# A gated cross-attention and expert layer on Trainium2: all four down tiles of a quad moved in front of its last two products

## The chip, the cores and the metric

The kernel runs on one core of a Trainium2 chip. The core has a matrix engine (TensorE, PE in the profile, with its weight loads as PEld), VectorE (DVE), ScalarE (ACT), GpSimd (POOL) and SyncE (SP), which issues most of the DMA. Each engine works through its own list of instructions in order and waits on semaphores where it needs another's result. The metric is the device time of one execution in microseconds; lower is better.

## The reference

What is computed, cut to what matters here (8 sequences of 256 tokens, width 512; 8 expert groups with 352 inner features each):

```python
x = x + tanh(g_xattn[0]) * xattn(layernorm(x), ctx, ctx, wq, wk, wv, wo)      # keys: 256 context + 256 own tokens
x = x + tanh(g_ffn[0]) * ffn(layernorm(x), ...)

def ffn(x):                                     # x: 2048 tokens x 512
    scores = softmax(x @ gate_w.T)              # 64 experts
    topk_w, topk_idx = top_k(scores, 8)
    w_e = zeros.at[rows, topk_idx].add(topk_w)
    flat = w_e[:, inv_map]                      # 8 groups of 8
    scalar = flat.sum(-1)
    soft = softmax(where(flat == 0, -1e9, flat), axis=-1)
    xg = x[:, None, :] + einsum('ngi,ghi->ngh', soft, mask_up_w)
    g = einsum('ngh,gih->ngi', xg, gate_proj_w)
    u = einsum('ngh,gih->ngi', xg, up_proj_w)
    d = einsum('ngi,ghi->ngh', silu(g) * u, down_proj_w)
    return einsum('ng,ngh->nh', scalar, d)
```

All matrix products are made from operands split into a high and a low part, three matmuls (low by high, high by low, high by high) per block of 128.

## The kernel before

The attention part and the router run first, one sequence at a time, up to about 340 us. Then comes the expert part, in which the change lies. It has two passes over 1024 tokens each. A pass has eleven units, a unit is two quads, so there are 44 quads (0 to 43; 0 to 21 are the first pass, 22 to 43 the second). One quad takes 128 inner features of the gate and of the up projection for two chunks of 512 tokens. The four half-size block products of either are made with seven products in place of eight, by sums and differences of weights and tokens. Each of the seven is six matmuls of 128x128 by 128x512 (line 1605).

**A quad on TensorE.** Products 1 and 6, in the first pass eight small matmuls for the masked stack (line 1619), products 2, 5 and 7, two small-stack matmuls (line 1611, "soft"), product 4 with a soft matmul, product 3 with a soft matmul. Beside them each quad carries four of the eight down tiles of the unit before it (line 76, six matmuls each): an even quad tiles 0 to 3, an odd one tiles 4 to 7. `early_tiles` says how many of these four stand behind the soft pair, in front of product 4; the rest stand behind product 3. Before the change that is two and two. Quads 0, 1, 2 and 43 have none early.

**What the other engines do with it.** There are two sets of buffers and PSUM banks, for even and odd quads.
- ScalarE copies product 1 out of PSUM (`first_sum`, line 921; product 2 waits for it), makes the two silus (lines 977 and 997), and rounds weights (line 796) and activations (`act_high`, line 889) to their high halves. At an even quad it also rounds the down weights (line 904).
- VectorE adds the products (lines 1316, 1348, 1355, 1398, 1404), multiplies (1401, 1413) and scales (line 1297), adds each down tile to the residual (`add_down`, line 1304), and in the first pass masks the small stack (lines 1277 to 1288) and does the router's steps for the last sequences. `add_down` of a tile stands where the tile does: early ones in front of the wait for product 4, of the late ones the third tile's behind line 1404 and the fourth's behind the last scaling.
- GpSimd makes weight sums (lines 640 to 645), the low halves of the weights (649), of the down weights (694) and of the activations (`act_low`, line 699), and in quads 11, 13, 15 and 17 sums of a piece of the tokens (lines 658 to 667).
- SyncE loads the weights of quad q + 2 once the last low half of quad q is made, and stores the router's scalars (line 429) in quads 2, 9 and 14, in one queue with the loads.

**What waits for what around the change.** The last group of a quad's weights is rounded on ScalarE only when the previous quad's product 3 is done, and in the first pass the small matmuls wait for its low half. Product 5 waits for line 1277, the soft pair for line 1288. The first down tile of an even quad waits for the low halves of the down weights and of an activation block (`act_low` of the quad before), and each down tile waits for the residual add two tiles before it, as there are two PSUM banks for them.

Of the kernel before, what the change touches and what calls it, by code (L numbers as in the profile page):

```python
# [28 lines left out]
QUADS = 2 * UNITS  # L29
# [31 lines left out]

def early_tiles(q):

    return 0 if q <= 2 or q == QUADS - 1 else 2


def split_products(hi_l, lo_l, hi_r, lo_r, tiles):
# [52 lines left out]
def layer_program(nc, x, ctx_nat, ctx_t, w_qkvo, w_gate_up, w_down, mask_up, gate_t, inv_map, gains, out):  # L120
    with ExitStack() as stack:
# [119 lines left out]
        early = Zone(a.at)  # L241
# [157 lines left out]
        def _(sp):  # L399
# [56 lines left out]
            def store_piece(i):  # L456
                _, _, at = piece_tokens(i)
                sp.wait_ge(s_piece_lo, i + 1)
                for dram, part in ((th_dram, sums_hi), (tl_dram, sums_lo)):
                    sp.dma_start(dram[:, :, :, at:at + PIECE].rearrange("p t k n -> p (t k) n"),  # L460
                                 f32(part[piece_home(i)][:]).rearrange("p c k n -> p (c k) n")).then_inc(s_piece_out, 16)
# [542 lines left out]
        def _(dve):  # L1004
# [286 lines left out]
            def scaled(quad, c, part):  # L1291

                q = quad.q
                dve.wait_ge(s_prod, 2 * q + c + 1)
                if quad.p == 0:
                    dve.wait_ge(s_scal_in[quad.j], 16 * HALF_G * (quad.s + 1))
                nc.vector.tensor_tensor(part, part, scalars[:, quad.j, c], ALU.mult).then_inc(s_act, 1)  # L1297

            def add_down(n):

                u, t = divmod(n, UNIT_TILES)
                row = xres[:, u // PAIRS * UNIT_TILES + t, :]
                dve.wait_ge(s_down, n + 1)
                nc.vector.tensor_tensor(row, row, bank[6 + t % 2][:], ALU.add).then_inc(s_res, 1)  # L1304
# [14 lines left out]
            for quad in quads:  # L1319
                q = quad.q  # L1320
                sums = tmp[quad.set]
                psum_b, psum_c = bank[BANKS[quad.set][1]], bank[BANKS[quad.set][2]]
                below = 4 * (q - 2)
                early = early_tiles(q)

                if q != 1:
# [85 lines left out]
                dve.wait_ge(s_c22, q + 1)  # L1412
                nc.vector.tensor_tensor(sums[:, SUM_3], sums[:, SUM_3], sums[:, SUM_2], ALU.mult).then_inc(s_prod, 1)  # L1413
                scaled(quad, 1, sums[:, SUM_3])
                if q >= 2:
                    add_down(below + 3)
            for n in range(UNIT_TILES * (UNITS - 1), UNIT_TILES * UNITS):
                add_down(n)
# [2 lines left out]
        def _(pe):  # L1421
# [266 lines left out]
            def soft_products(quad):  # L1688
                q, s, j = quad.q, quad.s, quad.j
                psum_a, _, psum_c = banks_of(quad)  # L1690
                if s == 0:
                    pe.wait_ge(s_a_st, q + 1)
                else:
                    pe.wait_ge(s_a_in[j], 16 * (quad.p + 1))
                if quad.p == 0:
                    pe.wait_ge(s_soft_in[j], 16 * (s + 1))
                soft_product(psum_c, quad, UP, 1).then_inc(s_m5, 1)
                soft_product(psum_a, quad, GATE, 0).then_inc(s_c11, 1)
# [50 lines left out]
            for quad in quads[2:]:  # L1749
                q = quad.q  # L1750
                below = 4 * (q - 2)
                early = early_tiles(q)
                product_1(quad)
                product_6(quad)
# [100 lines left out]
```

## Time and profile before

| | |
|---|---|
| median of 3 runs | 1096.89 us (1096.8 to 1097.58) |
| the profiled execution's own time | 1099.27 us |
| its span, first to last instruction | 1097.5 us |
| TensorE busy | 1056.5 us, 96% |
| VectorE / ScalarE / GpSimd busy | 746.9 / 379.8 / 634.1 us |
| mean granted TensorE clock | 0.989 of full speed |
| HBM read and written | 79 MB and 32 MB |

The span is about 1.8 us shorter than that execution's time, and the execution is 2.4 us longer than the median of the runs. A busy share says how much an engine works, not whether its results come in time: in an ordered queue one late result stops all behind it.

### The profile page before, as it was taken

What the parts mean: (1) busy time and instruction counts of PE and PEld (TensorE: products, weight loads), DVE (VectorE), ACT (ScalarE), POOL (GpSimd) and SP (SyncE); (2) the same over time, 40 slices, a digit from 0 to 9 for tenths busy, and PEclk for the clock granted to TensorE, in tenths of its full rate; (3) what the DMA queues carried; (4) which work ended last, traced back from release to release, by engine and by line L of the source; (5) the groups of instructions that cost most, each with busy time, mean ns of one, the idle gap of its engine ahead of it and who ended that gap; (6) DMA issues with size and microseconds to landing.
All of it is one profiled execution on the core that took longest, in us unless ns stands there. A gap on an engine that the chain in (4) does not pass through costs nothing.

```text
span 1097.5 us, 14456 instructions
## 1 busy us (share of the span) xinstructions
PE 1056.5 (96%) x5388; PEld 895.8 (82%) x5388; DVE 746.9 (68%) x1320; ACT 379.8 (35%) x635; POOL 634.1 (58%) x511
## 2 busy tenths in 40 slices
PE   7999999999999869999999999999999999999998
PEld 7889988988887657888877788878888888888886
DVE  7775665766667845878788988746656655665665
ACT  4333323433323333334244333323233333323331
POOL 0212203533515826866888888756777776677761
PEclk8999999999999998999999999999999999999999
DMA  9112225356685252023332633294322112212202
GB/s 333 61 40 96 60 47 145 65 157 164 176 249 176 77 54 73 28 81 46 92 104 60 125 110 121 80 324 137 105 73 72 43 57 73 72 47 71 72 27 77
DMA packets 114134, 111.64 MB, mean 102 GB/s; under 512 B 20881, under 2 KB 96401, under 8 KB 114065
## 3 DMA queue, kind: packets, MB, share of 16 engines
q1 hardware_dynamic: 113696, 110.58, 35.2%
q8 instruction: 43, 0.70, 0.3%
q14 instruction: 27, 0.21, 0.1%
q10 hardware_dynamic: 368, 0.15, 0.1%
HBM read 79.05 MB, written 31.65 MB: 101 GB/s over the span
## 4 chain that ended last, share of the span: by engine, by line
PE 76%; DVE 12%; DMA 3%; issue 3%; SPq 2%; ACT 2%; POOL 1%; DVEq 0%; ACTq 0%
PE bank L76 40%; PE bank L1605 29%; PE bank L1611 3%; PE bank L1438 1%; DVE a_stack L1288 1%; DVE tmp L1297 1%; DMA wgu_raw<-in_w_gate_up 1%; PE bank L1619 1%; SPq L460 1%; DVE tmp L1413 1%; DVE xres L1304 1%; DMA x2t<-token_sums_l 1%; DVE tmp L1401 1%; DVE a_stack L1286 1%; DVE soft L1137 1%
## 5 line engine op out<-in xcount | busy, mean ns | idle before, releaser
L1605 PE MATMUL bank<-x2t,wgu_hi 128*128 128x512 f32 x1144 | 354.2, 391 | 0.0
L649 POOL TENSOR_TENSOR wgu_lo<-wgu_raw,wgu_hi 128x512 fp32r<-128x512 f32 (+1 forms) x129 | 210.4, 1637 | 97.5 <-ACT wgu_hi L796 95.8
L1605 PEld LDWEIGHTS bank<-x2t,wgu_hi 128*128 128x128 f32 x1144 | 215.7, 189 | 44.4
L1605 PE MATMUL bank<-x2t,wgu_lo 128*128 128x512 f32 x572 | 225.6, 394 | 5.6 <-DMA x2t<-token_sums_l 2.7
L796 ACT CAST wgu_hi<-wgu_raw 128x512 fp32r<-128x512 f32 (+1 forms) x129 | 93.7, 727 | 231.4 <-PE bank L1611 188.9
L1304 DVE TENSOR_TENSOR xres<-xres,bank 128x512 f32<-128x512 f32 x176 | 120.0, 682 | 54.6 <-PE bank L76 54.5
L1605 PEld LDWEIGHTS bank<-x2t,wgu_lo 128*128 128x128 f32 x572 | 107.9, 189 | 30.6 <-issue 4.9
L76 PE MATMUL bank<-wd_hi,at_second 128*128 128x512 f32 x336 | 130.8, 389 | 0.0
L76 PE MATMUL bank<-wd_hi,at_first 128*128 128x512 f32 x256 | 99.9, 390 | 2.4 <-issue 2.4
L1297 DVE TENSOR_TENSOR tmp<-tmp,scalars 128x512 f32<-128x512 f32 x88 | 99.1, 1127 | 3.0
L1348 DVE TENSOR_TENSOR tmp<-tmp,bank 128x512 f32<-128x512 f32 x44 | 30.2, 686 | 94.8 <-PE bank L1605 94.2
L694 POOL TENSOR_TENSOR wd_lo<-wd_raw,wd_hi 128x512 fp32r<-128x512 f32 x42 | 54.2, 1312 | 54.2 <-ACT wd_hi L904 54.2
L76 PE MATMUL bank<-xnt_hi,w_lo_qkv 128*128 128x256 f32 x256 | 75.0, 293 | 2.6 <-DVE xnt_lo L1049 2.6
L76 PEld LDWEIGHTS bank<-wd_hi,at_second 128*128 128x128 f32 x336 | 63.1, 188 | 13.3
L76 PE MATMUL bank<-xnt_hi,w_hi_qkv 128*128 128x256 f32 x256 | 73.6, 288 | 0.0
L76 PE MATMUL bank<-xnt_lo,w_hi_qkv 128*128 128x256 f32 x256 | 73.6, 287 | 0.0
L1611 PE MATMUL bank<-soft_t,a_stack 128*128 128x512 f32 x176 | 62.9, 398 | 3.5 <-DVE a_stack L1288 3.4
L977 ACT ACTIVATE tmp<-bank 128x512 f32<-128x512 f32 x44 | 26.3, 599 | 114.2 <-PE bank L1611 114.2
L76 PE MATMUL bank<-wd_lo,at_second 128*128 128x512 f32 x168 | 65.4, 389 | 0.0
L699 POOL TENSOR_TENSOR at_second<-tmp,at_second 128x512 fp32r<-128x512 f32 x44 | 59.9, 1380 | 5.7 <-ACT at_second L889 5.7
L699 POOL TENSOR_TENSOR at_first<-tmp,at_first 128x512 fp32r<-128x512 f32 x33 | 45.3, 1374 | 29.1 <-ACT at_first L889 29.1
L76 PEld LDWEIGHTS bank<-wd_hi,at_first 128*128 128x128 f32 x256 | 48.2, 188 | 13.7 <-issue 2.8
(213 smaller groups left out, 2253.5 us busy)
## 6 DMA issues: line engine op xcount, KB each, us to landing
wgu_raw<-in_w_gate_up SPq DMA_DIRECT2D x43, 512.0 KB, 4.2
wd_raw<-in_w_down SPq DMA_DIRECT2D x22, 512.0 KB, 4.9
a_stacks<-a_stack SPq DMA_DIRECT2D x22, 192.0 KB, 1.9
a_stack<-a_stacks SPq DMA_DIRECT2D x22, 192.0 KB, 4.0
ctxt_raw<-in_ctx_t SPq DMA_DIRECT2D x8, 512.0 KB, 11.7
ctx_raw<-in_ctx SPq DMA_DIRECT2D x8, 512.0 KB, 9.4
x<-x_raw SPq DMA_DIRECT2D x8, 512.0 KB, 4.0
sums_raw<-x SPq DMA_DIRECT2D x16, 256.0 KB, 3.9
```

What stands on the lines that cost most here:

```text
L76: last = nc.tensor.matmul(out, stationary, moving, start=n == 0, stop=n == len(pairs) - 1)
L460: sp.dma_start(dram[:, :, :, at:at + PIECE].rearrange("p t k n -> p (t k) n"), f32(part[piece_home(i)][:]).rearrange("p c k n -> p (c k) n ...
L649: nc.gpsimd.tensor_tensor(wgu_lo[:, group], raw_of(quad)[:, group], f32(wgu_hi[:, group]), ALU.subtract).then_inc(s_fw_lo, 1)
L694: nc.gpsimd.tensor_tensor(lo[:, j], wd_raw[:, j], f32(hi[:, j]), ALU.subtract).then_inc(s_wd_lo, 1)
L699: nc.gpsimd.tensor_tensor(lo, tmp[quad.set][:, SUM_3 if c else ACTED], f32(hi), ALU.subtract).then_inc(s_at_lo, 1)
L796: nc.scalar.copy(wgu_hi[:, group], raw_of(quad)[:, group]).then_inc(s_fw_hi, 1)
L977: nc.scalar.activation(sums[:, ACTED], psum_a[:], ACT.Silu).then_inc(s_silu_0, 1)
L1297: nc.vector.tensor_tensor(part, part, scalars[:, quad.j, c], ALU.mult).then_inc(s_act, 1)
L1304: nc.vector.tensor_tensor(row, row, bank[6 + t % 2][:], ALU.add).then_inc(s_res, 1)
L1348: nc.vector.tensor_tensor(sums[:, SUM_3], sums[:, SUM_1], psum_b[:], ALU.add).then_inc(s_s3, 1)
L1605: last = nc.tensor.matmul(out_bank[:], stationary, moving, start=begins and n == 0, stop=n == len(pairs) - 1, skip_group_check=True)
L1611: return nc.tensor.matmul(out_bank[:], a_stack[:, quad.j, m, :], soft_t[:, quad.j, c, :], start=False, stop=True, skip_group_check=True)
```

## The change

`early_tiles` returns 4 instead of 2 for the quads 3 to 42. On TensorE tiles 3 and 4 of the quad go in front of products 4 and 3; on VectorE their residual adds go in front of the wait for product 4, and the add that stood behind the last scaling is made only where the quad has no four early tiles. ScalarE's, GpSimd's and SyncE's lists are the same as before.

```diff
 def early_tiles(q):
-    return 0 if q <= 2 or q == QUADS - 1 else 2
+    return 0 if q <= 2 or q == QUADS - 1 else 4
@@ VectorE, behind the last scaling of a quad
-                if q >= 2:
+                if q >= 2 and early < 4:
                     add_down(below + 3)
```

TensorE before, in the second pass, from the soft matmul of product 4 in an even quad on: product 3 (line 1605), its soft matmul, then the third down tile (line 76; at_first and at_second are the two activation blocks, wd_hi and wd_lo the down weights).

```order
L1611 MATMUL bank<-soft_t,a_stack 128x512
L1605 MATMUL bank<-x2t,wgu_lo 128x512 [waits c22_done]
L1605 MATMUL bank<-x2t,wgu_hi 128x512 x2
L1605 MATMUL bank<-x2t,wgu_lo 128x512
L1605 MATMUL bank<-x2t,wgu_hi 128x512 x2
L1611 MATMUL bank<-soft_t,a_stack 128x512
L76 MATMUL bank<-wd_hi,at_first_154 128x512 [waits residual_done]
L76 MATMUL bank<-wd_lo,at_first_154 128x512
```

The same place now; x2t_spare is the token block of the next quad's product 1.

```order
L1611 MATMUL bank<-soft_t,a_stack 128x512
L1605 MATMUL bank<-x2t,wgu_lo 128x512 [waits c22_done]
L1605 MATMUL bank<-x2t,wgu_hi 128x512 x2
L1605 MATMUL bank<-x2t,wgu_lo 128x512
L1605 MATMUL bank<-x2t,wgu_hi 128x512 x2
L1611 MATMUL bank<-soft_t,a_stack 128x512
L1605 MATMUL bank<-x2t_spare,wgu_lo 128x512 [waits wgu_lo_done,silu0_done]
L1605 MATMUL bank<-x2t_spare,wgu_hi 128x512 x2
```

Behind the last matmul of product 3 the next quad's product 1 follows at once; the twelve matmuls of two down tiles that stood between them are gone from here.

VectorE before, in quad 42 of the second pass and the sum that follows it:

```order
L1355 TENSOR_TENSOR tmp_140<-tmp_140,bank 128x512 [waits m5_ready,sum3_done]
L1304 TENSOR_TENSOR xres<-xres,bank 128x512 [waits down_ready] x2
L1398 TENSOR_TENSOR tmp_140<-tmp_140,bank 128x512 [waits m4_ready]
L1401 TENSOR_TENSOR tmp_140<-tmp_140 128x512 [waits silu0_done,c21_done]
L1297 TENSOR_TENSOR tmp_140<-tmp_140,scalars 128x512 [waits prod_done]
L1404 TENSOR_TENSOR tmp_140<-tmp_140,bank 128x512 [waits m3_ready]
L1304 TENSOR_TENSOR xres<-xres,bank 128x512 [waits down_ready]
L1413 TENSOR_TENSOR tmp_140<-tmp_140 128x512 [waits c22_done,silu1_done]
L1297 TENSOR_TENSOR tmp_140<-tmp_140,scalars 128x512 [waits prod_done]
L1304 TENSOR_TENSOR xres<-xres,bank 128x512 [waits down_ready]
L1316 TENSOR_TENSOR tmp_141<-tmp_141,bank 128x512 [waits m6_ready,sum1_done]
```

and now:

```order
L1355 TENSOR_TENSOR tmp_140<-tmp_140,bank 128x512 [waits m5_ready,sum3_done]
L1304 TENSOR_TENSOR xres<-xres,bank 128x512 [waits down_ready] x4
L1398 TENSOR_TENSOR tmp_140<-tmp_140,bank 128x512 [waits m4_ready]
L1401 TENSOR_TENSOR tmp_140<-tmp_140 128x512 [waits silu0_done,c21_done]
L1297 TENSOR_TENSOR tmp_140<-tmp_140,scalars 128x512 [waits prod_done]
L1404 TENSOR_TENSOR tmp_140<-tmp_140,bank 128x512 [waits m3_ready]
L1413 TENSOR_TENSOR tmp_140<-tmp_140 128x512 [waits c22_done,silu1_done]
L1297 TENSOR_TENSOR tmp_140<-tmp_140,scalars 128x512 [waits prod_done]
L1316 TENSOR_TENSOR tmp_141<-tmp_141,bank 128x512 [waits m6_ready,sum1_done]
```

The residual adds stand in a row of four in front of the wait for product 4, and none is left between the wait for product 3 and the next quad's first sum.

## Rows read from the trace of the kernel before

**Rows 1.** One stretch, the second pass: busy time of each engine, clock, DMA.
```profile
732.00:1080.00 348.00, 344.88 (x1507) 283.36 (x1506) 211.69 (x280) 116.91 (x192) 247.99 (x211) 1.00 0.23 77
```

**Rows 2.** Chain that ended last, in quad 27: start, length, what.
```profile
824.29 2.72 PE bank L76 x12
```

**Rows 3.** Timeline (start, length, engine, line), quad 27's last matmul to quad 28's first tile.
```profile
823.90 0.39 PE L1611 MATMUL bank<-soft_t,a_stack 128*128 128x512 f32 x1
...
825.39 0.68 DVE L1404 TENSOR_TENSOR tmp<-tmp,bank 128x512 f32<-128x512 f32 x1
...
827.49 0.69 DVE L1297 TENSOR_TENSOR tmp<-tmp,scalars 128x512 f32<-128x512 f32 x1
...
828.44 0.59 ACT L921 COPY tmp<-bank 128x512 f32<-128x512 f32 x1 [1.71 <-PE bank L1605]
828.93 0.62 ACT L889 CAST at_second<-tmp 128x512 fp32r<-128x512 f32 x1
...
830.15 2.54 POOL L694 TENSOR_TENSOR wd_lo<-wd_raw,wd_hi 128x512 fp32r<-128x512 f32 x2 [3.52 <-ACT wd_hi L904]
832.65 2.54 POOL L699 TENSOR_TENSOR at_second<-tmp,at_second 128x512 fp32r<-128x512 f32 x2
...
834.17 0.40 PE L76 MATMUL bank<-wd_hi,at_first 128*128 128x512 f32 x1
```

**Rows 4.** Timeline, behind the last matmul of quad 26.
```profile
807.96 0.39 PE L1611 MATMUL bank<-soft_t,a_stack 128*128 128x512 f32 x1
...
810.08 0.63 ACT L997 ACTIVATE tmp<-tmp 128x512 f32<-128x512 f32 x1 [1.06 <-DVE tmp L1404]
...
811.16 0.62 ACT L889 CAST at_first<-tmp 128x512 fp32r<-128x512 f32 x1 [0.46 <-PE bank L76]
...
811.86 1.29 POOL L699 TENSOR_TENSOR at_first<-tmp,at_first 128x512 fp32r<-128x512 f32 x1 [0.57 <-ACT at_first L889]
811.87 1.83 DVE L1297 TENSOR_TENSOR tmp<-tmp,scalars 128x512 f32<-128x512 f32 x1
```

**Rows 5.** Timeline, small matmuls and VectorE's mask in quad 21.
```profile
712.50 0.28 PE L1619 MATMUL bank<-wgu_hi,mu 128*128 128x256 f32 x1
...
713.09 0.67 DVE L1316 TENSOR_TENSOR tmp<-tmp,bank 128x512 f32<-128x512 f32 x1
...
713.45 0.40 PE L1605 MATMUL bank<-x2t,wgu_lo 128*128 128x512 f32 x1
...
713.69 0.41 DVE L1277 TENSOR_TENSOR a_tmp<-bank,group_mask 128x256 f32<-128x256 f32 x1
```

**Rows 6.** Timeline, last matmul of quad 7 and VectorE's add of it.
```profile
478.85 0.39 PE L1611 MATMUL bank<-soft_t,a_stack 128*128 128x512 f32 x1
...
481.90 0.68 DVE L1404 TENSOR_TENSOR tmp<-tmp,bank 128x512 f32<-128x512 f32 x1
```

**Rows 7.** Timeline of GpSimd, first and last operation of a token piece.
```profile
586.43 1.19 POOL L658 TENSOR_TENSOR sums_raw<-sums_raw 128x256 f32<-128x256 f32 x1
...
589.68 1.07 POOL L667 TENSOR_TENSOR sums_raw<-sums_raw 128x256 f32<-128x256 f32 x1
```

**Rows 8.** Timeline, the load for quad 5 and quad 4's wait.
```profile
396.49 0.60 SPq L438 DMA_DIRECT2D wgu_raw<-in_w_gate_up  x1
...
409.57 0.72 POOL L640 TENSOR_TENSOR wgu_raw<-wgu_raw 128x256 f32<-128x256 f32 x1 [15.05 <-DMA wgu_raw<-in_w_gate_up]
...
413.83 0.55 PE L1619 MATMUL bank<-wgu_hi,mu 128*128 128x256 f32 x1 [11.26 <-POOL wgu_lo L649]
```

**Rows 9.** Waits of TensorE over the span: us in total, times, longest.
```profile
PE bank L1611 <- DVE a_stack L1288: 3.4, 7, 1.3
```

**Rows 10.** Timeline of TensorE behind two waits.
```profile
377.32 0.47 PE L76 MATMUL bank<-wd_hi,at_first 128*128 128x512 f32 x1 [2.39 <-issue]
...
734.99 0.68 PE L1605 MATMUL bank<-x2t,wgu_lo 128*128 128x512 f32 x1 [2.70 <-DMA x2t<-token_sums_l]
...
738.46 0.41 PE L76 MATMUL bank<-wd_hi,at_first 128*128 128x512 f32 x1
```

## The prediction

> **What bounds the kernel now.** I read the stretches first, then the critical chain of one quad, then the timeline of all engines around the end of a quad's last product. In the stretch of the second pass TensorE is busy 344.9 of 348 us at the full clock while the Vector, Scalar and GpSimd engines are busy 212, 117 and 248 us [rows 1]. So matmul issue bounds this stage: the twelve matmuls of two down tiles take 2.72 us, or 0.227 us each [rows 2]. No other engine is short of time in sum; whether one of them is late at some point of a quad is a question of slack, and that is where the change acts. The number of matmuls stays the same, so TensorE can win nothing but waits that exist now, and it has few.
>
> **What is moved.** For quads 3 to 42 the third and fourth down tile leave the place behind product 3 and go in front of product 4. The last product of a quad then ends directly where the next quad begins: two down tiles, 2.72 us, of cover behind product 3 are gone. Call t0 the start of the last matmul of a quad's product 3. Everything that hangs on that product (ScalarE's second silu, the last product and scaling on VectorE, the split of the activation, and what stands behind these in the queues) had 2.72 us more before the next quad's waits than it will have. VectorE also loses two residual adds behind product 3 and gets them in front of the wait for product 4, where it was idle.
>
> **Even quads, second pass.** The first down tile of an even quad waits for the low half of the down weights and of one activation block. Behind t0 = 823.90, VectorE adds product 3 at 825.39, then silu, product and scaling; the scaling ends at 828.18, 4.28 behind t0 [rows 3]. In this trace ScalarE takes that only after the copy of the next quad's first product at 828.44, so the activation split starts at 828.93, 5.03 behind t0. From there the work is a chain: split, copies of the down weights behind it in ScalarE's queue, two subtractions on GpSimd from 830.15, the subtraction of the activation from 832.65 (half of 2.54, to 833.92), and the tile at 834.17: 5.24 us from the split's start to the tile. The tile is at t0 + 10.27 with nothing waiting. After the change it could start at t0 + 10.27 - 2.72 = 7.55. The copy on ScalarE comes 2.72 earlier too and ends at t0 + 2.4 by its own row, but the scaling does not come earlier: it hangs on product 3, and the adds that leave VectorE's queue stood in its wait for silu. So the split starts at t0 + 4.33, and the tile at 4.33 + 5.24 = 9.57. TensorE waits 2.0 us. This holds for each of ten even quads (24 to 42): 20.2 us. Below, 1.5 if the weight copies overlap better than in the row; above, 2.6 if the two subtractions meet VectorE.
>
> **Odd quads, second pass.** Here ScalarE's order behind product 3 is silu, split, copy of the next quad's first product, and product 2 waits for that copy. Behind t0 = 807.96 silu starts at 810.08, t0 + 2.12, when VectorE has added product 3. The split now waits for the fourth down tile [rows 4]; that wait goes away, but the split itself stays in the queue. Starting 0.5 us apart as ScalarE's operations do when none waits (copy and split of rows 3, 828.44 and 828.93), the split starts at 2.62 and the copy at 3.12, which ends 0.59 later at 3.71. Product 2 would start thirteen matmuls behind t0, at 2.95, and starts some 0.15 behind the copy (an estimate; rows 3 show 0.25 from 833.92 to 834.17), at 3.86: 0.91 us, eleven quads (23 to 43), 10.0 us. Below 0.4, above 1.2.
>
> **First pass.** Eight small matmuls more stand in front of product 2 (0.95 us from 712.50 to 713.45) [rows 5], so product 2 would start at 3.9 and its wait is gone, but product 5 waits for VectorE's mask of that small result. Quad by quad:
> - Odd quads: scaling, the next quad's sum and the mask follow each other on VectorE. Where GpSimd subtracts the activation at the same time, the scaling takes 1.83 instead of 0.69 us [rows 4]. It would be over at t0 + 5.3, the sum (0.67) at 5.9, the mask (0.41) at 6.25, and product 5 starts at 6.4 instead of 5.3. That is 1.1 for four quads (5, 7, 11, 21). In the other five (9, 13, 15, 17, 19) routing work or a piece of the token sums delays VectorE by 0.9 to 1.6 us, of which the small stack tile's present waits already pay a part: 1.7 each. Sum 12.9. Below 0.15 a quad, if VectorE gets its operand before GpSimd; above 2.4.
> - Even quads: as in the second pass, less the 0.95 of the small matmuls, less what transposes and present waits stand there: 0.6, 0.5 and 1.2 in quads 6, 10 and 20. In front of quad 8, VectorE's add starts 3.05 us behind t0 (478.85 to 481.90) and not 1.5 [rows 6], which leaves 1.9. In front of quads 12, 14, 16 and 18 GpSimd first makes the sums of a token piece, four operations from 586.43 to 590.75 [rows 7], and only then turns to the down weights; with these the first tile is ready at about t0 + 11.1 where it is wanted at about 8.9: 2.2 each, 8.7. Sum 12.9. Below 0.4 a quad, above 2.4.
> - Quad 4: TensorE waits 11.26 us now, until the low half of the weights is there. That chain runs back to a load which GpSimd has at 409.57. SyncE issued it at 396.49 [rows 8], behind the store of the routing scalars in its queue, and VectorE makes these scalars after its early adds. Two more adds stand in front of them, each behind its down tile: the store and the load go 2.72 us later, and the wait grows by 2.7. In quads 9 and 14 the same store moves; no product waits for the loads behind it now, and I take nothing for them (at most 2.7 each).
> - Quad 22: it waits 2.70 us for token blocks [rows 10]. The loads are bound by the queue and start behind the small stack tile of quad 21, which comes about 2 us later against TensorE: 2.0.
>
> The Trainium skill (SBUF — State Buffer, section "SBUF: two separate sides") says that VectorE and GpSimd share one port pair as an exclusive lock: whichever starts first keeps it for the whole instruction. By that rule the odd quads of the first pass keep their 1.1 us; if there were no such lock they would wait 0.15, and the sum would be 8.6 us smaller. The scaling of 1.83 us beside GpSimd's 1.29 agrees with the lock.
>
> **The sum.** 2.7 + 12.9 + 12.9 + 2.0 + 20.2 + 10.0 = 60.7 us. On the profiled execution's 1099.3 us that is 1160.0; the median of the runs lies 2.4 lower, at 1096.9, so I predict 1158. Nothing is to be set against it: TensorE's waits for the small stack tile are 3.4 us in the whole kernel [rows 9], and those hang on the same late VectorE.
>
> **Rivals.**
> - Faster. The two adds that leave VectorE's queue behind product 3 (0.68 each) shorten its chain by 1.36, the small stack tile comes earlier and its waits (3.4 us) go: 1096.9 - 3.4 = 1093.5. It decides if the scaling comes out so early that product 3 to first tile takes under 7.55 us. Against it: the chain of rows 3 adds up to 9.57, and in even quads the first of the two adds ran while silu was awaited. 3%.
> - Only the late scalars. The queues have slack that the rows hide, quads lose nothing, and the store costs 2.7: 1099.6. 6%.
> - Odd quads don't wait: ScalarE's copy gets through and VectorE wins against GpSimd. 60.7 - 10.0 - 12.9 = 37.8: 1134.7. For it: the spacing of 0.5 and the order of two operations that start within 0.02 us are all that these terms have. 15%.
> - The clock falls as well. Behind the wait of 2.70 us eight matmuls take from 734.99 to 738.46, 0.434 each and not 0.227, half the clock, so this wait costs 1.66 us on top. Behind the one of 2.39 us the clock did not fall [rows 10]. If waits of 2 us do it too, ten to twenty even quads cost 16.6 to 33.2 us more: 1174 to 1191. 12%.
>
> **How the numbers follow.** My forecast gets 64%, with a range of its own from 1143 to 1172 (the low ends of half the terms, the high ends of half). The range for 8 in 10 leaves out the two small rivals and the upper part of the clock's, and takes in the odd quads' rival: 1134 to 1176. A difference of 0.2%, 2.2 us, is about what can be told from no change. Slower by more than that: forecast, odd quads, clock and most of the late scalars, 94%. Faster 3%, within 3%.
>
> **What would show it.** Right: in each even quad of the second pass the first down tile's matmul is released by GpSimd's subtraction after some 2 us of idle time, and ScalarE's split waits for VectorE's scaling; in odd ones product 2 is released by ScalarE's copy. In the first pass product 5 waits for the mask in odd quads. The load for quad 5 is issued at about 399, and quad 4's wait is near 14. VectorE's adds stand in fours with no wait of TensorE between tiles. Wrong: TensorE gapless in the second pass, or half clock there, or waits at the down tiles for the residual adds.

## The result, and the profile after

The changed kernel takes 1142.01 us (median of 4 runs, 1141.01 to 1143.18), the kernel before 1096.85 beside it: 1.0415 times as long, 95% interval 1.0397 to 1.0433, or 45 us more. The profiled execution took 1141.01 us, its span is 1139.2 us. Of the four runs of the kernel with both orders, below, one fell in the chip's slow state (1504.12 us at a mean clock of 0.653 of full speed) and is left out there.

Page of the changed kernel, busy times; then one stretch of its second pass, with the columns of rows 1:

```profile
PE 1068.8 (94%) x5388; PEld 892.4 (78%) x5388; DVE 733.9 (64%) x1320; ACT 371.8 (33%) x635; POOL 604.5 (53%) x511
```
```profile
780.00:1110.00 330.00, 317.35 (x1372) 255.58 (x1370) 180.90 (x256) 102.24 (x176) 212.57 (x194) 1.00 0.19 63
```

TensorE stands still 12.7 of 330 us here, where it stood still 3.1 of 348 [rows 1], at the full clock. Over the span VectorE and GpSimd are busy less than before, and TensorE's busy time is 12.3 us longer for the same number of matmuls: no engine got more work, and most of what was added is waiting. TensorE's waits over the span (us in total, times, longest):

```profile
PE bank L76 <- issue: 18.2, 17, 2.4
PE bank L1619 <- POOL wgu_lo L649: 13.9, 1, 13.9
PE bank L1611 <- DVE a_stack L1288: 7.3, 11, 1.3
PE bank L1605 <- DVE a_tmp L1277: 6.6, 13, 0.9
PE bank L1605 <- ACT tmp L921: 3.8, 13, 1.1
PE bank L1605 <- DMA x2t<-token_sums_l: 3.6, 1, 3.6
```

The first row is the first down tile (one such wait of 2.4 us before, now 17 waits), the fourth is product 5 behind the mask (1.7 us before), the fifth product 2 behind ScalarE's copy (none before), the third the small stack tile [rows 9].

**Second pass, even quad.** Timeline behind the last matmul of quad 27's product 3, the place of rows 3:

```profile
853.70 0.39 PE L1611 MATMUL bank<-soft_t,a_stack 128*128 128x512 f32 x1
...
854.59 0.68 DVE L1404 TENSOR_TENSOR tmp<-tmp,bank 128x512 f32<-128x512 f32 x1
...
856.70 0.69 DVE L1297 TENSOR_TENSOR tmp<-tmp,scalars 128x512 f32<-128x512 f32 x1
...
857.43 0.63 ACT L889 CAST at_second<-tmp 128x512 fp32r<-128x512 f32 x1 [1.01 <-DVE tmp L1297]
857.96 1.13 ACT L904 CAST wd_hi<-wd_raw 128x512 fp32r<-128x512 f32 x2
...
858.65 2.53 POOL L694 TENSOR_TENSOR wd_lo<-wd_raw,wd_hi 128x512 fp32r<-128x512 f32 x2 [2.53 <-ACT wd_hi L904]
...
861.13 2.52 POOL L699 TENSOR_TENSOR at_second<-tmp,at_second 128x512 fp32r<-128x512 f32 x2
...
862.51 0.47 PE L76 MATMUL bank<-wd_hi,at_first 128*128 128x512 f32 x1 [1.08 <-issue]
862.82 0.40 PE L76 MATMUL bank<-wd_lo,at_first 128*128 128x512 f32 x1
```

The chain is the forecast one: scaling, split, weights behind it, GpSimd, tile. The tile starts at t0 + 8.81, where 7.55 was wanted: 1.26 us late, and the matmul behind it follows 0.31 us later, not 0.227. Together 1.34 us; by the length of the quad it is 1.36.

**Second pass, odd quad,** behind quad 26's product 3, the place of rows 4:

```profile
837.29 0.39 PE L1611 MATMUL bank<-soft_t,a_stack 128*128 128x512 f32 x1
...
838.91 0.64 ACT L997 ACTIVATE tmp<-tmp 128x512 f32<-128x512 f32 x1 [0.56 <-DVE tmp L1404]
...
839.45 0.60 ACT L889 CAST at_first<-tmp 128x512 fp32r<-128x512 f32 x1
...
839.95 0.57 ACT L921 COPY tmp<-bank 128x512 f32<-128x512 f32 x1
840.13 1.28 POOL L699 TENSOR_TENSOR at_first<-tmp,at_first 128x512 fp32r<-128x512 f32 x1 [0.42 <-ACT at_first L889]
840.30 1.65 DVE L1297 TENSOR_TENSOR tmp<-tmp,scalars 128x512 f32<-128x512 f32 x1
...
840.67 0.47 PE L1605 MATMUL bank<-x2t,wgu_lo 128*128 128x512 f32 x1 [0.20 <-ACT tmp L921]
```

Product 2 waits for the copy (line 921), which stands behind the split (line 889); it starts at t0 + 3.38, where 2.95 was wanted.

**First pass,** quad 21 (the place of rows 5) and quad 4 (the place of rows 8):

```profile
732.11 1.67 DVE L1297 TENSOR_TENSOR tmp<-tmp,scalars 128x512 f32<-128x512 f32 x1
...
734.30 0.41 DVE L1277 TENSOR_TENSOR a_tmp<-bank,group_mask 128x256 f32<-128x256 f32 x1
...
734.76 0.50 PE L1605 MATMUL bank<-x2t,wgu_lo 128*128 128x512 f32 x1 [0.21 <-DVE a_tmp L1277]
```
```profile
394.71 0.23 DVE L1148 TENSOR_SCALAR scal_out<-scal,gain 128x16 f32<-128x16 f32 x1
...
396.29 0.60 SPq L438 DMA_DIRECT2D wgu_raw<-in_w_gate_up  x1
...
413.57 0.55 PE L1619 MATMUL bank<-wgu_hi,mu 128*128 128x256 f32 x1 [13.93 <-POOL wgu_lo L649]
```

The load for quad 5 is issued at 396.29; that profile was 2.9 us ahead of before's at the end of quad 2, so on before's time this is 399.2. Quad 4 waits 13.93 us, not 11.26.

**The whole by quads.** A quad's length is taken from the last matmul of one product 3 to that of the next. Sums of the differences against before: quad 4 +2.9; even quads 6 to 20 +9.5; odd quads 5 to 21 +11.1; quad 22 +2.4; even quads 24 to 42 +13.6 (each 1.33 to 1.39); odd quads 23 to 43 +5.2 (0.45 to 0.49 each). That is all of the 44.7 us between the ends of quads 2 and 43; 2.7 us more in quad 3 and 2.7 less in quad 43 are the two tiles themselves, which change sides of the mark.

### The profile page after: what moved, and what is told of

Same layout as the page of the kernel before. It is cut to its first block, busy times and chain, and to the rows that moved or that the text cites. A ratio compares the mean times of both kernels' runs of the same rounds, so it can differ in the third digit from the quotient of the medians.

```text
span 1139.2 us, 14456 instructions
## 1 busy us (share of the span) xinstructions
PE 1068.8 (94%) x5388; PEld 892.4 (78%) x5388; DVE 733.9 (64%) x1320; ACT 371.8 (33%) x635; POOL 604.5 (53%) x511
## 4 chain that ended last, share of the span: by engine, by line
PE 71%; DVE 15%; issue 6%; ACT 3%; DMA 3%; POOL 2%; SPq 1%; DVEq 0%; ACTq 0%
PE bank L76 44%; PE bank L1605 21%; PE bank L1611 3%; DVE a_stack L1286 2%; PE bank L1438 2%; DVE tmp L1401 1%; DVE tmp L1398 1%; DVE tmp L1404 1%; DMA wgu_raw<-in_w_gate_up 1%; DVE a_stack L1288 1%; DVE a_tmp L1280 1%; DVE tmp L1413 1%; DMA x2t<-token_sums_l 1%; DVE tmp L1316 1%; DVE tmp L1297 1%
## 5 line engine op out<-in xcount | busy, mean ns | idle before, releaser
L649 POOL TENSOR_TENSOR wgu_lo<-wgu_raw,wgu_hi 128x512 fp32r<-128x512 f32 (+1 forms) x129 | 204.0, 1588 | 177.5 <-ACT wgu_hi L796 177.5
L1605 PE MATMUL bank<-x2t,wgu_lo 128*128 128x512 f32 x572 | 228.2, 399 | 15.1 <-DVE a_tmp L1277 6.6
L1297 DVE TENSOR_TENSOR tmp<-tmp,scalars 128x512 f32<-128x512 f32 x88 | 87.2, 991 | 3.0
L76 PEld LDWEIGHTS bank<-wd_hi,at_second 128*128 128x128 f32 x336 | 63.4, 189 | 13.5
L699 POOL TENSOR_TENSOR at_first<-tmp,at_first 128x512 fp32r<-128x512 f32 x33 | 42.5, 1289 | 29.1 <-ACT at_first L889 29.1
## 6 DMA issues: line engine op xcount, KB each, us to landing
ctxt_raw<-in_ctx_t SPq DMA_DIRECT2D x8, 512.0 KB, 11.5
```

Of the source, the lines that this page charges most:

```text
L76: last = nc.tensor.matmul(out, stationary, moving, start=n == 0, stop=n == len(pairs) - 1)
L649: nc.gpsimd.tensor_tensor(wgu_lo[:, group], raw_of(quad)[:, group], f32(wgu_hi[:, group]), ALU.subtract).then_inc(s_fw_lo, 1)
L699: nc.gpsimd.tensor_tensor(lo, tmp[quad.set][:, SUM_3 if c else ACTED], f32(hi), ALU.subtract).then_inc(s_at_lo, 1)
L1605: last = nc.tensor.matmul(out_bank[:], stationary, moving, start=begins and n == 0, stop=n == len(pairs) - 1, skip_group_check=True)
```

## The experiments

Ratios are against the kernel before, run on the same chip in turn. Its median was 1100.05 us beside the first four experiments and 1095.99 or 1096.90 beside the others, so where two experiments are compared by their times the quads' lengths in the traces are the surer measure. "q" is a quad.

### The second pass alone

```diff
-    return 0 if q <= 2 or q == QUADS - 1 else 4
+    return 0 if q <= 2 or q == QUADS - 1 else 2 if q < QUADS // 2 else 4
```

> Four early tiles in quads 22 to 42 only; quads 3 to 21 as before the change. My account by quads (measured between the ends of product 3): ten even quads of the second pass lost 1.36 us each, eleven odd ones 0.48, the rest 25.9 us lies in quads 4 to 22. Then this kernel is 18.8 us slower than before: 1115.7. Rival, that the loss of a quad is carried on from the first pass (late transfers, clock): under 8 us, below 1105.

Measured: 1118.47 us beside 1100.05, ratio 1.0173 (1.0153 to 1.0193), 19 us. Even quads 1.36 each, odd 0.48, the first pass as before. Quad 22 is 2.7 longer by the two tiles' own move and nothing else. The two passes are separate costs: these 19 us and the 25.9 of quads 4 to 22 in the changed kernel add up to the whole.

### Three tiles early

```diff
-    return 0 if q <= 2 or q == QUADS - 1 else 4
+    return 0 if q <= 2 or q == QUADS - 1 else 3
```

> Three tiles early, one late. With one tile (1.36 us) of cover behind product 3 the first tile of an even quad is wanted at t0 + 8.91 and was ready at 8.81 in the changed kernel. If the adding of product 3 stays at t0 + 0.9 as there, nothing is lost in the second pass, quad 4 loses 1.4, quads with token pieces about 0.5 each: about 1101. If it goes back to t0 + 1.49 as before the change, ten even quads lose 0.5 more: 1106. Rival, that the loss is in proportion to the tiles moved: half of 45, 1119.

Measured: 1115.11 us, ratio 1.0146 (1.0129 to 1.0163), 16 us. In the second pass as expected: 0.04 us an even quad, nothing in odd ones. The rest was a miss, as some 1101 us were expected: quads 3 and 4 lose 3.4 beside the tile's own move, not 1.4, and quads 5 to 21 of the first pass 11.0 us, the largest of them 3.6 in quad 9. There the fourth tile's add, which stays behind the last scaling, holds up a transpose of the router, and 3.4 us at half the clock follow:

```profile
506.62 1.64 DVE L1297 TENSOR_TENSOR tmp<-tmp,scalars 128x512 f32<-128x512 f32 x1
508.19 0.68 DVE L1304 TENSOR_TENSOR xres<-xres,bank 128x512 f32<-128x512 f32 x1
...
508.92 0.64 PE L1503 MATMUL bank<-ident,rest 128*64 128x128 f32 x2 [2.05 <-DVE xres L1304]
```

The cost is not proportional to the tiles moved: it starts where the cover behind product 3 falls below the chain, at another place in each pass.

### ScalarE: weights ahead of the split

The changed kernel, with the down weights rounded ahead of the activation split in even quads.

```diff
-                if q >= 1:
-                    act_high(quads[q - 1], 1)
                 if quad.j == 0 and u >= 2:
                     down_weights(u - 1)
+                if q >= 1:
+                    act_high(quads[q - 1], 1)
```

> Changed kernel, but ScalarE rounds the down weights in front of the split of the last activation block, so the GpSimd chain to the first down tile no longer hangs on VectorE's scaling. My theory: the copies start at t0 + 2.7 and not 4.3, the tile is ready at about 7.3 where it is wanted at 7.5, the even quads of the second pass win 1.36 each and plain ones of the first pass some 0.5: about 1142 - 15 = 1127. Quads 12, 14, 16, 18 stay, as GpSimd's token pieces end later. Rival, that the tile waits for the residual adds or PSUM banks: no change, 1142.

Measured: 1125.56 us, ratio 1.0231 (1.0216 to 1.0247). By the ratios 20 us of the 46 are gone, by the quads of the two traces 16.3 of 44.7, of which 13.8 lie in the even quads of the second pass; 15 were expected. Quad 28 of that kernel; its t0 is 849.34:

```profile
851.96 1.14 ACT L904 CAST wd_hi<-wd_raw 128x512 fp32r<-128x512 f32 x2
...
852.66 2.78 POOL L694 TENSOR_TENSOR wd_lo<-wd_raw,wd_hi 128x512 fp32r<-128x512 f32 x2 [0.90 <-ACT wd_hi L904]
853.08 0.62 ACT L889 CAST at_second<-tmp 128x512 fp32r<-128x512 f32 x1
...
855.39 2.54 POOL L699 TENSOR_TENSOR at_second<-tmp,at_second 128x512 fp32r<-128x512 f32 x2
...
856.89 0.39 PE L76 MATMUL bank<-wd_hi,at_first 128*128 128x512 f32 x1
```

GpSimd no longer idles behind the split, and the tile starts at t0 + 7.55 with no wait. All ten even quads lost their 1.36, odd ones kept 0.5. The even quads' wait was the order of ScalarE's queue, and of GpSimd's behind it, not work.

### ScalarE: the copy ahead of the split

The changed kernel, with `first_sum` of odd quads from 5 on ahead of `act_high`.

```diff
+                if after and q >= 4 and quad.j == 0:
+                    first_sum(after)
                 if quad.j == 0:
                     act_high(quad, 0)
```

> Changed kernel, but in front of odd quads (5 to 43) ScalarE copies the next product 1 ahead of the activation split. My theory: product 2 no longer waits (11 x 0.48 = 5.3), and GpSimd's subtraction starts 0.5 later, behind the start of VectorE's scaling, which then takes 0.7 and not 1.7, so product 5 in the first pass starts up to 0.9 earlier in nine quads (4 to 8 us): 1129 to 1133. Rival, that product 7's wait for the sum takes the place of product 2's: 1140 to 1142.

Measured: 1129.55 us, ratio 1.0275 (1.0249 to 1.0301), 15 us gone by the ratios. Odd quads of the second pass: 0.00 over before, each. Odd quads of the first pass fell from 11.1 to 2.8: with the copy first GpSimd's subtraction starts later, VectorE's scaling gets there ahead of it and ends at t0 + 3.70, not 4.66. That is 13.5 us by the quads. The profiled execution, the slowest of the four (1134.12 us), shows only 7.1 in all: its quads 12 and 16 are 1.6 and 2.2 longer than in the changed kernel, each with 3.4 us at half the clock, and quad 3 is 3.3 longer. So the rival "odd quads don't wait" was a matter of an order of two instructions, 0.5 us apart.

### Both orders

The changed kernel with both edits. Their diffs are those above.

> The changed kernel with both queue orders of the two earlier runs: ScalarE rounds the down weights ahead of the activation split in even quads, and in odd quads from 5 on copies product 1 ahead of the split. Theory: the two take away different waits, so they add up. The changed kernel stood at 1.0415 of before; the weights' order gave back 0.018, the copy's order 0.014; together about 1.009 to 1.010, some 10 us over before, of which quad 4 2.9, quad 22 2 and the rest in the first pass; second pass: even quads 0.0, odd quads 0.0 us over before. Rival (the two share a wait, so only the larger counts in a unit): 1.018 to 1.023, with 0.5 us or more left in odd quads of the second pass.

Measured: 1109.74 us (three runs), ratio 1.0119 (1.0101 to 1.0137), 13 us over before. The two add up but for 0.003, which is within the intervals; quad 12 fell to half the clock here (3.5 us over before, 1.9 in the changed kernel), which is 0.0015. One stretch of its second pass, and then VectorE and GpSimd behind quad 26's last product 3 (t0 = 822.49):

```profile
760.00:1085.00 325.00, 325.00 (x1429) 267.07 (x1427) 178.05 (x265) 109.17 (x184) 225.96 (x199) 1.00 0.20 68
```
```profile
825.50 0.69 DVE L1299 TENSOR_TENSOR tmp<-tmp,scalars 128x512 f32<-128x512 f32 x1
825.81 1.53 POOL L699 TENSOR_TENSOR at_first<-tmp,at_first 128x512 fp32r<-128x512 f32 x1 [0.89 <-ACT at_first L889]
```

TensorE has no gap left there, and of VectorE and GpSimd it is now the latter, second to start, that takes longer (1.53 us, and 1.28 in the changed kernel). What remains is the first pass (10.9 us), quad 4 (2.5) and quad 22 (2.3).

### VectorE's contention: the sums later

The kernel before, with one edit on GpSimd.

```diff
-                    if 3 <= q < QUADS - 2:
-                        weight_sums(quads[q + 2])
                     weight_low(after, 2, GROUP_C)
-                    if q < 3:
+                    if q < QUADS - 2:
                         weight_sums(quads[q + 2])
```

> The kernel before (two down tiles early), with one edit: GpSimd makes the weight sums for quad q+2 behind the low half of the last weight group and not in front of it, so that they no longer run beside VectorE's product and scaling ahead of its add of product 3. Theory (why the forecast was too long): that add stood at t0+1.49 only because two VectorE instructions in front of it ran longer beside GpSimd (0.86 and 1.12 us against 0.69). Without the sums beside them the add starts at t0+0.90, where product 3 is ready, and the scaling in even quads of the second pass ends 0.6 us earlier. The time of the whole stays within 0.3% of before in the second pass, since two tiles of cover hide it; what GpSimd makes later there may cost in the first pass. Rival (the add's time is set by product 3 or by the semaphore): the add stays at t0+1.4 to 1.5.

Measured: one run, 1105.56 us, so no interval. The second pass is within 0.02 us a quad of before. At the end of quad 27 (t0 = 830.23) the product and the scaling ahead of the add take 0.69 us each, and the add starts 0.89 behind t0; behind every product 3 from quad 23 to quad 41 it is 0.90 or within 0.01 of it:

```profile
829.79 0.69 DVE L1399 TENSOR_TENSOR tmp<-tmp 128x512 f32<-128x512 f32 x1
830.51 0.69 DVE L1295 TENSOR_TENSOR tmp<-tmp,scalars 128x512 f32<-128x512 f32 x1
831.12 0.68 DVE L1402 TENSOR_TENSOR tmp<-tmp,bank 128x512 f32<-128x512 f32 x1
```

That settles why the add was late in the trace of before. The expected gain of 0.6 us at the scaling was a miss: GpSimd's sums now stand beside the product and scaling behind the add (1.28 and 1.12 us there in place of 0.69), and the scaling ends at t0 + 4.2 to 4.8. The loss lies in the first pass's even quads (11.7 us, most of it in quads 12 to 18, where GpSimd now comes late to the down weights); quad 4 gives 3.6 back.

### Quad 4: the scalars between the adds

The changed kernel; in quad 3 VectorE makes the routing scalars between the second and the third add.

```diff
                 for n in range(early):
+                    if q == 3 and n == 2:
+                        route_scalars(B - 3)
                     add_down(below + n)
```

> The changed kernel with one edit on VectorE: in quad 3 the routing scalars of a sequence are made between the second and the third residual add, not behind all four. Theory: quad 4 waits 2.7 us longer than before only because the third and fourth add stand in front of these scalars, each behind its down tile, and the store and the load of quad 5's weights follow them in SyncE's queue. So quad 3 to quad 4 loses the 2.9 us again (with the clock up to 4 us), all other quads stay as in the changed kernel within 0.1 us: 1138 to 1139 us beside 1142. Rival (the load is late because TensorE releases the weight buffer later): quad 4 stays 2.9 us over before.

Measured: one run, 1135.99 us. Quad 4 goes from +2.9 to -0.4 us, its wait from 13.9 to 11.0. The other quads stay as they were, but for quad 16 (+1.6, a stretch at half the clock) and quad 22 (1.0 less). The predicted reason holds, shown by that one trace; 2.2 us of the total are this run's quicker early stage.

### Quad 4: the store behind the loads

The kernel before, with SyncE's store one quad later, behind the loads.

```diff
                 if q == 2:
                     store_x2(B - 1, x2r_hi, x2r_lo)
+                if q == 3:
                     store_scalars(B - 3)
```

> The kernel before (two down tiles early), with one edit: SyncE's store of a sequence's routing scalars is issued one quad later, behind the weight loads and not in front of them. Theory: quad 4's wait of 11.26 us is there because the loads of its weights stand behind the store in SyncE's queue, and the store waits for VectorE's scalars. With the store behind them the load that was issued at 396.49 comes several us earlier; quad 4's wait falls below 1 us, and the half clock behind it (10.2 us at half speed, about 5 us of cost) goes too: 11 to 15 us faster, ratio 0.986 to 0.990. Rival (the load is late for another reason, the buffer's release or GpSimd's own queue): the wait stays over 8 us, ratio 0.997 to 1.0. Second rival: the wait moves to quad 5 or 6, where the store now stands in front of another load: ratio 0.99 to 0.995 with a new wait there.

Measured: 1084.35 us beside 1095.99, ratio 0.9888 (0.9873 to 0.9904), 12 us faster than before. The load of quad 5's weights, issued at 396.49 before [rows 8], and GpSimd's first sum of them:

```profile
377.08 0.59 SPq L438 DMA_DIRECT2D wgu_raw<-in_w_gate_up  x1
...
394.27 0.73 POOL L641 TENSOR_TENSOR wgu_raw<-wgu_raw 128x256 f32<-128x256 f32 x1
```

The wait of 11.26 us is gone, quad 4 is 12.2 us shorter, and no quad behind it got longer. Quad 3 is 3.4 us longer and quad 2 2.6 shorter in this trace, behind 3.4 us at half the clock in quad 1. That is not the store's: the copy-first kernel, whose store is in its old place, has the same (3.3 and 2.6, and the half clock in quad 1), and the two-early kernel of the next step, whose store is moved, has a quad 3 as before.

### All of it, four early and two early

Two kernels with both ScalarE orders and the store behind the loads; the second has, against the first:

```diff
-    return 0 if q <= 2 or q == QUADS - 1 else 4
+    return 0 if q <= 2 or q == QUADS - 1 else 2
```

> All four down tiles early, with both ScalarE orders and the store of the scalars behind the loads: does the placement of the changed kernel win anything once its waits are gone? Theory: the number of matmuls is the same and no wait is shorter with four early tiles, so at best it is level with the kernel before that has only the store later; the first pass keeps 3 to 6 us of new waits (the mask in odd quads, the weight sums' quads 12 to 18). 1.009 less the store's 0.012: ratio 0.994 to 1.000, and 2 to 8 us slower than two early tiles with the store later. Rival (four early tiles shorten VectorE's chain behind product 3 and win once ScalarE's order is right): faster than that kernel by 2 us or more.

> The kernel before (two down tiles early) with the store of the scalars behind the loads and both ScalarE orders: the same edits as in the four-early kernel that stood at 1.002, with early_tiles back at 2. Theory: with two tiles of cover behind product 3 nothing in the second pass waits, so the two orders win nothing: within 0.2% of the kernel with the store later alone (0.989), each quad of the second pass within 0.05 us. So the 13 us between the four-early kernel and this one belong to the place of the tiles: the first pass and quad 22. Rival (the orders themselves help or hurt by over 2 us): 0.986 or below, or 0.992 and above.

Four early: 1098.73 us, ratio 1.0020 (1.0008 to 1.0032). That is 14 us behind the kernel with the store later alone, and 2 to 8 were expected: the first pass stays 10.0 us over before, not 3 to 6. Two early: 1082.73 us, ratio 0.9866 (0.9846 to 0.9885), the fastest kernel of the study. So with every wait of the second pass mended the place of the tiles costs 1.5%, 17 us; by quads: even ones of the first pass 9.3 us, odd ones 4.4, quads 3 and 4 2.7 more beyond the tiles' own move, quad 22 0.8, the second pass nothing. Some 3 us of that (quads 3 and 12) are stretches at half the clock in the four-early trace. Two early with the orders beats two early without them by 3.8 us in the odd quads of the first pass (quads 13 to 19 0.9 each), though the two ratios' intervals overlap.

### GpSimd: the token pieces behind the down weights

The four-early kernel of the last step; in quads 12, 14, 16, 18 the piece's sums go behind the low halves, and ScalarE rounds the piece behind its second weight group (that part of the edit is not shown).

```diff
                     act_low(quads[q - 1], 1)
+                if q in (12, 14, 16, 18):
+                    piece_sums(PIECES + (q - 12) // 2)
 ...
-                    if q in (11, 13, 15, 17):
-                        piece_sums(PIECES + (q - 11) // 2)
```

> The changed kernel with both ScalarE orders and the store of the scalars behind the loads, and one edit more: in quads 12, 14, 16 and 18 GpSimd makes the four sums of a token piece behind the low halves of the down weights and activations, not in front of them, and ScalarE rounds the piece after its second weight group. Theory: the 0.9 to 1.8 us that quads 12, 14, 16 and 18 still wait for their first down tile are the 3.8 us of these sums in front of the down weights; with them behind, the four quads are at 0 to 0.3 us over before, and the half clock in quad 12 (1.6 us) goes: 6 to 7 us faster than without this edit (which stood at 1.002), ratio 0.996 to 0.997. Rival (the wait is VectorE's, or the small stack tile's): the first down tiles stay over 1 us late and the ratio stays 1.001 to 1.003.

Measured: 1098.95 us, ratio 1.0021 (1.0011 to 1.0031): no change. That is the ratio that the rival named, but not for its reason. The four even quads did lose their waits (7.9 us over before, now 1.7 under it), and the four odd ones behind them took as much: quad 13 stands at +1.9 where it stood at -1.0, quads 15, 17 and 19 at +2.8 to +3.2 where they stood at +0.3. Quad 13 of that kernel:

```profile
560.20 1.71 POOL L650 TENSOR_TENSOR wgu_lo<-wgu_raw,wgu_hi 128x512 fp32r<-128x512 f32 x1
...
562.06 0.36 PE L1622 MATMUL bank<-wgu_hi,mu 128*128 128x256 f32 x1 [1.86 <-POOL wgu_lo L650]
```

The weights' low half is late now. Two tiles of cover had paid for the piece; without them it has no free place in these units' queue that was tried.

## Why the prediction was right and where it was wrong

| term | predicted | measured |
|---|---|---|
| quad 4 | 2.7 | 2.9 |
| even quads, first pass | 12.9 | 9.5 |
| odd quads, first pass | 12.9 | 11.1 |
| quad 22 | 2.0 | 2.4 |
| even quads, second pass | 20.2 | 13.6 |
| odd quads, second pass | 10.0 | 5.2 |
| sum | 60.7 | 44.7 |

- **Sign, places and releasers were right.** All six terms are there, with the releasers named. The time, 1142.0, is 1 us below the forecast's own range, which began at 1143. It lies in the range of 8 in 10 only because that one reached down to 1134 for a rival, odd quads that don't wait, and they did wait in both passes: that is luck.
- **The step that failed** is the start of the chain: "Behind t0 = 823.90, VectorE adds product 3 at 825.39", carried over with "the scaling does not come earlier: it hangs on product 3". I took t0 + 1.49 for the time at which product 3 is ready. It was VectorE's own queue. Two rows of GpSimd and two of VectorE in the kernel before, ahead of that add:

```profile
823.03 0.74 POOL L643 TENSOR_TENSOR wgu_raw<-wgu_raw 128x256 f32<-128x256 f32 x1
823.46 0.86 DVE L1401 TENSOR_TENSOR tmp<-tmp 128x512 f32<-128x512 f32 x1
823.85 1.07 POOL L645 TENSOR_TENSOR wgu_raw<-wgu_raw 128x256 f32<-128x256 f32 x1
824.35 1.12 DVE L1297 TENSOR_TENSOR tmp<-tmp,scalars 128x512 f32<-128x512 f32 x1
```

The product and the scaling take 0.86 and 1.12 us beside GpSimd's sums; the scaling ends at 825.47, and the add follows it with no gap. After the change the two down tiles stand ahead of product 4, VectorE's product falls 2.7 us later against GpSimd, which is done with the sums, and both run in 0.69; in the changed kernel, ahead of t0 = 853.70 and the add at 854.59:

```profile
853.26 0.69 DVE L1401 TENSOR_TENSOR tmp<-tmp 128x512 f32<-128x512 f32 x1
853.98 0.69 DVE L1297 TENSOR_TENSOR tmp<-tmp,scalars 128x512 f32<-128x512 f32 x1
```

The grouped rows of that product in before and then in after (count, busy us, mean ns, idle before) show it over the kernel:

```profile
L1401 DVE TENSOR_TENSOR tmp<-tmp 128x512 f32<-128x512 f32 x44 | 38.0, 863 | 1.5
```
```profile
L1401 DVE TENSOR_TENSOR tmp<-tmp 128x512 f32<-128x512 f32 x44 | 31.6, 717 | 1.5
```

At t0 + 0.89, too, the add follows the scaling with no gap. Product 4's add, which does wait for TensorE, starts 0.43 behind the start of that product's last matmul (852.54 and 852.11 in the changed kernel); by that, an estimate, product 3 is ready at about t0 + 0.43. So in both kernels the chain begins at product 4, with three VectorE operations ahead of the add of product 3.

- **What it was worth.** The add comes at t0 + 0.89, the split in even quads at 3.73 and not 4.33, silu in odd ones at 1.62 and not 2.12. The rest of the even chain took 5.08, not 5.24. So 1.26 us in place of 2.02, and 0.43 in place of 0.91; the slower first matmul behind the wait, which I had left out, adds 0.08 each. Together that is 11.4 of the 16.0 us of error: the late start of the chain 11.5, its rest 1.6, the matmuls 1.7 the other way. The run with the sums later shows the same add at 0.89 in the kernel before, so the cause is tested and not only argued.
- **First pass.** The same 0.6 us is missing from quads 6 and 10 (0.15 each, predicted 0.6 and 0.5) and partly from the odd ones (quad 5 0.3, predicted 1.1). The piece's quads cost 6.3 us (1.9, 0.9, 1.8, 1.8), predicted 8.7; quad 8 2.0 (predicted 1.9). Quads 7 and 11 cost 1.5 and 1.9 where I had 1.1: in the run with both orders, where the mask's wait is mended, they still lose 0.9 each, with a wait of 0.54 for the small stack tile. What sets that tile there was not tried.
- **Quad 22** was near by luck. Its wait grew by 0.9 (2.70 to 3.63 us), where I had 2.0, and the clock, for which I had nothing, gave the rest. The wait is as long, 3.75 and 3.87 us, in the kernel with the sums later and in the two-early kernel with all orders, so more than the place of the tiles sets it; no run was made for it alone.
- **The lock.** The scaling beside GpSimd's subtraction takes 1.65 and 1.67 us, against 0.69 alone, and ends 0.5 us behind that subtraction's end (841.41 in the odd quad's rows). With the copy first, VectorE gets there before GpSimd and takes 0.69, while GpSimd takes 1.53 and not 1.28: who starts first decides. The rule of the Trainium skill (SBUF — State Buffer, section "SBUF: two separate sides"), an exclusive lock for the whole instruction, agrees with both in who is held up; VectorE's scaling, 0.69 us long alone, ends 0.54 us behind GpSimd's end, so 0.15 us less than a wait for the whole instruction would give. The same rule spoke for the cause of the error above, and I had not applied it to the rows ahead of the add.
- **The clock** did not fall behind the second pass's waits (1.08 us long by their rows), as forecast. It fell for longer where waits were there before: quad 4 (13.7 us at half, 10.2 before) and quad 22 (6.8, 3.4 before); the 3.4 us more at half the clock cost 1.7 us there. Elsewhere in the first pass of the changed kernel it stayed at full.

## What to carry to other kernels

An instruction's start in a trace is the time its queue let it go, not the time its input was ready: before a start is carried over to a changed schedule, read the rows ahead of it on its own engine, and whether another engine had lengthened them. Work that seems to cost nothing between two products can be the cover for the slowest chain behind the first; moving it earlier costs the chain's length less the cover that is left, nothing down to a threshold and then all of it (three tiles early 0.04 us a quad in the second pass, four 1.36). And the largest single wait of a tuned kernel can be one queue's order: a store in front of a load was 12 us.

## What the runs showed that was not expected

The same wait can leave TensorE's clock alone or halve it. Quad 12's first down tile waits 1.68 us in the changed kernel and 1.70 us in the four-early one with all orders. The stretch of 3.4 us ahead of that tile and the one just behind it, in the changed kernel and then in the other (the clock is the third column from the end):

```profile
566.37:569.77 3.40, 1.70 (x7) 0.78 (x6) 2.31 (x3) 2.29 (x4) 3.40 (x4) 1.00 0.16 58
570.20:573.60 3.40, 3.40 (x17) 2.80 (x16) 1.37 (x2) 0.00 (x0) 3.40 (x3) 1.00 0.00 0
```
```profile
545.95:549.35 3.40, 1.66 (x7) 0.76 (x6) 2.29 (x3) 2.28 (x4) 3.40 (x4) 1.00 0.16 58
549.80:553.20 3.40, 3.40 (x10) 2.62 (x9) 0.69 (x1) 0.00 (x0) 3.40 (x3) 0.50 0.00 0
```

TensorE did the same ahead of both, 1.70 and 1.66 us of work, and behind it got through 17 matmuls in one and 10 in the other: 1.6 us of difference. Over all the traces, waits of 1.68 to 1.70 us for the first down tile of quad 12 or 16 occur nine times, and 3.4 us at half the clock begin within 1 us of the wait's end in six of them. What decided it these rows don't show, so a forecast can give the clock's price of such a wait only a chance, and two kernels that differ elsewhere can differ by it: 2.64 us of wait at quad 22 left the clock alone in the kernel with the store later, and 2.70 halved it before [rows 10].
